# Cross-attention in eight chunks of keys a head: maxima in even steps, shifts computed on GpSimd, sums copied later

## The reference, cut to what matters

```python
q, k = _fq_sym(q, axis=-1), _fq_sym(k, axis=-1)      # 8-bit steps
v = _fq_sym(v, axis=2)
attn = softmax(einsum('bhqd,bhkd->bhqk', q, k))      # 16 heads, 896 queries, 24000 keys
attn = _fq_unsigned(attn, axis=-1)                   # round(255 * attn / max) * max / 255
out = einsum('bhqk,bhkd->bhqd', attn, v) @ Wp + bp
```

## Time and profile before

| | |
|---|---|
| median of 3 runs | 4739.06 us (4736.8 to 4739.14) |
| the profiled execution | 4743.85 us, its span 4740.7 us |
| TensorE clock granted | 0.986 of full over the span, 1.00 in the attention |
| busy over the span | PE 96%, VectorE 87%, ScalarE 76%, GpSimd 78% |
| one call of 192 steps | 221.2 to 223.4 us (14 calls from 966.5 to 4074.0 us) |

### The profile page before, as it was taken

How to read it: one execution, slowest core, us unless ns; L and a number is a source line. 1 busy time by engine, 2 the same in 40 slices (tenths; PEclk the granted TensorE clock), 3 DMA queues, 4 the chain that set the end, 5 groups by cost and what they waited for, 6 DMA issues and landing times. The chain is left out here.

```text
span 4740.7 us, 153131 instructions
## 1 busy us (share of the span) xinstructions
PE 4551.2 (96%) x55123; PEld 2083.6 (44%) x55123; DVE 4121.6 (87%) x7608; ACT 3614.3 (76%) x4027; POOL 3682.4 (78%) x3920
## 2 busy tenths in 40 slices
PE   7999998999999999999999999999999999888999
PEld 5666663333334443334343433333333434334655
DVE  6788888999999999999999999999999999874333
ACT  3555557888888898889888989888898988883121
POOL 5777777888889888888898989888898989872000
PEclk9999998999999999999999999999999999998999
DMA  3555541111111111111111111111111111342000
GB/s 99 150 160 166 172 148 52 31 32 35 32 34 31 35 34 33 32 34 33 33 35 35 31 32 35 35 31 34 33 34 32 34 33 32 128 164 92 1 37 8
DMA packets 222786, 268.95 MB, mean 57 GB/s; under 512 B 34367, under 2 KB 202810, under 8 KB 221290
## 3 DMA queue, kind: packets, MB, share of 16 engines
q1 hardware_dynamic: 167529, 203.57, 15.4%
q10 hardware_dynamic: 54528, 55.60, 3.8%
HBM read 174.57 MB, written 82.97 MB: 54 GB/s over the span
## 5 line engine op out<-in xcount | busy, mean ns | idle before, releaser
L1563 ACT ACTIVATE e_home<-ps_scores,sk 125x896 f32<-125x896 f32 x3072 | 3053.8, 1007 | 331.1 <-ACTq L1557 194.9
L1599 DVE TENSOR_REDUCE unit_max<-ps_maxima 128x1 f32<-128x428 f32 (+1 forms) x5880 | 3167.9, 599 | 86.7 <-DVEq L1596 64.7
L1771 POOL TENSOR_SCALAR r<-e_home 125x896 f32<-125x896 f32 x2976 | 2774.2, 949 | 418.9 <-ACT e_home L1563 221.3
L1354 PE MATMUL ps_maxima<-e_home,zt 126*17 126x224 f32 x24576 | 1708.9, 353 | 1.0 <-issue 1.0
L1332 PE MATMUL ps_maxima<-k_home,q 48*128 48x428 bf16 (+1 forms) x5880 | 1619.4, 345 | 41.0 <-PEq L1331 1.9
L1308 PE MATMUL ps_scores<-q,k_home 54*128 54x448 bf16 x5760 | 1591.5, 356 | 19.3 <-PEq L109 6.9
L1349 PE MATMUL ps_maxima<-r,vt 125*16 125x224 f16 x12288 | 853.4, 267 | 29.9 <-PEq L1342 25.3
L1308 PEld LDWEIGHTS ps_scores<-q,k_home 54*128 54x128 bf16 x5760 | 357.0, 94 | 980.4 <-issue 819.0
L1332 PEld LDWEIGHTS ps_maxima<-k_home,q 48*128 48x128 bf16 x5880 | 540.5, 93 | 282.9 <-issue 143.0
L1354 PEld LDWEIGHTS ps_maxima<-e_home,zt 126*17 126x17 f32 x24576 | 628.2, 96 | 3.7 <-issue 2.7
L1349 PEld LDWEIGHTS ps_maxima<-r,vt 125*16 125x16 f16 x12288 | 296.7, 85 | 742.6 <-issue 742.0
(11 more groups left out here) (269 smaller groups left out, 3009.5 us busy)
## 6 DMA issues: line engine op xcount, KB each, us to landing
k_rows<-krows ACTq DMA_DIRECT2D x48, 1000.0 KB, 7.2
k_home<-k_rows SPq DMA_DIRECT2D x408, 93.8 KB
k_home<-k_rows SPq DMA_DIRECT2D x120, 281.2 KB
e_home<-in_ctxT SPq DMA_DIRECT2D x48, 500.0 KB, 4.2
vr<-v_raw SPq DMA_DIRECT2D x128, 187.5 KB
cb<-in_ctxT SPq DMA_DIRECT2D x16, 1500.0 KB, 6.1
v_raw<-e_home SPq DMA_DIRECT2D x12, 1000.0 KB
v_raw<-vb SPq DMA_DIRECT2D x12, 1000.0 KB
```

Of the source, the lines that this page charges most:

```text
L1354: last = pe.matmul(psav[c:c + WIDE, lo:hi], zt[u][0:ONES_ROW + 1, i + s, :], e[(i + s) % SLOTS][0:ONES_ROW + 1, g, lo:hi], start=False, st ...
L1563: act.activation(e[i % SLOTS][0:KT, :, :], score_banks(i)[0:KT, :, :], ACT.Exp, scale=sk[u][:, i:i + 1]).then_inc(e_wrote[h % 2], 1)
L1599: top = dve.tensor_reduce(unit_max[:, b, j * NPIECE + at:j * NPIECE + at + 1], ps[:, 0:CUTS[at + 1] - CUTS[at]], axis=AX.X, op=ALU.max)
L1771: pool.tensor_scalar(r[i % SLOTS][:, :, :], e[i % SLOTS][0:KT, :, :], 1.0, HALFWORD, ALU.mult, ALU.add)\
```

## The change

- The seventh block of queries takes six pieces of 500 keys instead of seven of 428, so a chunk has 48 pieces and a head 384 (`place` gives each piece its block and cut, the 500-wide ones are every eighth). The 12 last steps hold 22 of the next head's pieces instead of 12. 362 remain for 180 steps: two steps have three pieces, the others two (24 in the first call with three).
- The maxima have two tiles, one for each parity of the head.
- The shift's arithmetic (eight operations) goes from VectorE to GpSimd, behind the rounding of i = 13 of chunk 7. VectorE keeps the reduction of the maxima. TensorE turns the rows in two parts at i = 20 and 22, ahead of the scores, and ScalarE copies them ahead of the exponentials of those steps. The banks that they use are freed by ScalarE's semaphores.
- The values are scaled at i = 1 and 4, rounded at i = 7 and 10, and added up at i = 14, 16 and 18.
- At the change of head TensorE no longer waits for the last sums. ScalarE copies the sums after the exponential of i = 4, and step 5 has no sums. At i = 6 TensorE waits for the copy and does both halves of the first pair, the f32 products first with `start` set, so that no clearing is needed. Semaphore `e_free` for the old head's last pair is given by the first score of i = 5.

```diff
-SB = 428
-NPIECE = CK // SB
-CUTS = [a * SB for a in range(NPIECE)] + [CK]
+NPIECE, NLAST = 7, 6
+CUTS = [a * 428 for a in range(NPIECE)] + [CK]
+CUTS_LAST = [a * 500 for a in range(NLAST + 1)]
...
-    UNITS = NQB * NPIECE
+    UNITS = (NQB - 1) * NPIECE + NLAST
-    EARLY = (1, 0, 1, 0, 1, 1, 1, 1, 1, 1, 2, 2)
+    EARLY = (1, 2, 2, 2, 2, 2, 2, 2, 1, 2, 2, 2)
+    SHIFTED = 8, 10
-    TURNED = len(EARLY) // 2
-    SCALED, WHOLE = (5, 8), (SLOTS + 2, SLOTS + 5)
+    SCALED, WHOLE, CHAINED = (1, 4), (SLOTS - 1, SLOTS + 2), 13
-    SUMMED, SUMMED_FIRST = (19, 20, 21), (1, 2, 3)
+    SUMMED, SUMMED_FIRST = (14, 16, 18), (1, 2, 3)
...
+        def place(n):
+            j, k = divmod(n, UNITS)
+            if k % 8 == 1:
+                return j, NQB - 1, j * NLAST + k // 8, CUTS_LAST[k // 8], CUTS_LAST[k // 8 + 1]
+            at, b = divmod(k - (k + 6) // 8, NQB - 1)
+            return j, b, j * NPIECE + at, CUTS[at], CUTS[at + 1]
...
+            def bank_free():
+                pe.wait_ge(shift_banks.get(turn.used - len(ps1), s1_free), 1)\
+                  .then_inc(shift_banks.get(turn.used - len(ps1), s1_free), -1)
...
-                if head_end:
+                if head_first:
+                    exact()
+                    last = products()
+                else:
+                    products()
+                    last = exact()
+                if final:
                     pe_done(last)
                     pe.sem_inc(e_free, 2)
                     pe.sem_inc(sums_done, 1)
+                elif head_end:
+                    last.then_inc(sums_done, 1)
...
-                    if head_start and i == LAG:
+                    if head_start and at == 0:
                         if finished is not None:
                             sums_read()
-                        clear_sums()
-                    if at >= 0:
+                        else:
+                            clear_sums()
+                        sums(0, u, 0, shared=not first, head_first=True)
+                        sums(0, u, 1, shared=not first, head_first=True)
+                    elif at >= 0:
...
+            def copy_shifts(half, ps, y, pair):          # ScalarE
+                lo, hi = ((0, BANK), (BANK, TOK))[half]
+                act.wait_ge(shift_turned, 1).then_inc(shift_turned, -1)
...
+                copied = act.activation(q2[y][0:SROWS, lo:hi], ps[0:SROWS, 0:hi - lo], ACT.Copy)
...
+            def turn_shift(h1):                          # GpSimd
+                pool.wait_ge(max_ready, 1).then_inc(max_ready, -1)
+                pool_done(pool.tensor_tensor(shift[:, :], run_max[:, :],
+                                             sq[:, :, bass.ds(h1, 1)].rearrange("p b o -> p (b o)"), ALU.mult))
+                pool_done(pool.tensor_scalar(shift[:, :], shift[:, :], -1.0, LOG255, ALU.mult, ALU.add))
+                for part in range(2):
+                    pool_done(pool.tensor_copy(shift_parts[:, :, part], shift[:, :]))
+                    rest = shift[:, :] if part == 0 else shift_parts[:, :, 2]
+                    pool_done(pool.tensor_tensor(rest, shift[:, :], shift_parts[:, :, part], ALU.subtract))
+                pool_done(pool.tensor_copy(shift_parts[:, :, 3:5], shift_parts[:, :, 0:2]))
+                pool.tensor_copy(shift_parts[:, :, 5], shift_parts[:, :, 0]).then_inc(shift_ready, 1)
...
+                    if n % NCH == NCH - 1 and i == CHAINED and n // NCH < HEADS - 1:
+                        turn_shift(n // NCH + 1)
```

More of the change, by code:

```diff
@@ L1321, in piece @@
             def piece(n, y):
-                j, at, b = n // UNITS, n % UNITS // NQB, n % NQB
+                j, b, _, lo, hi = place(n)
                 u = j % 2
@@ L1372, in clear_sums, with shift_rows @@
                               start=True, stop=True, tile_position=(0, g * QUAD))
[L1374 to L1384 removed]
+            def shift_rows(half, places):
+                if half == 0:
+                    pe.wait_ge(shift_ready, 1).then_inc(shift_ready, -1)
+                ps, lo = turn.next(), 4 * half
+                bank_free()
+                shift_banks[turn.used] = q2_ready if half else shift_copied
+                for at in places:
+                    for b in range(lo, min(lo + 4, NQB)):
+                        last = pe.matmul(ps[at:at + SROWS, (b - lo) * QB:(b - lo + 1) * QB], shift_parts[:, b, :],
+                                         ident_b[:, :], start=True, stop=True, tile_position=(0, at))
+                last.then_inc(shift_turned, 1)
             def sum_values(i, u, part):
@@ L1500, in chunk @@
                             sum_values(i, u if own else 1 - u, part)
+                        if j * CT + i - MAIN in SHIFTED:
+                            shift_rows(SHIFTED.index(j * CT + i - MAIN), (0,) if more else (0, ROWS1))
                         if second:
-                            score(i, 0, u, 1 - y)
+                            score(i, 0, u, 1 - y, head_ended=head_start and i == LAG and finished is not None)
                         for ahead, n in todo[:-1]:
@@ L1572, in chunk @@
                 def chunk(j, u, head_start, last):
-                    if h2 is None:
-                        return
                     for i in range(CT):
+                        if h1 is not None and j * CT + i - MAIN in SHIFTED:
+                            copy_shifts(SHIFTED.index(j * CT + i - MAIN), turn.next(), y, not more)
+                        for _ in pieces(j * CT + i, finished is not None, more) if h1 is not None else ():
+                            turn.next()
                         scores(h2, j, i, u, not head_start or finished is not None,
                                summed_at(j, i, h1 is not None, True, finished, last))
-                        if head_start and finished is not None and i == LAG - 2:
+                        if head_start and finished is not None and i == LAG - 1:
                             copy_sums()
@@ L1731, in chunk @@
                         if first and step == MAIN:
-                            head_max(h1)
-                        if first and step == MAIN + 1:
-                            high_part()
-                        if first and step == MAIN + 3:
-                            other_parts()
+                            dve.tensor_reduce(run_max[:, :], maxima[y][:, :, :], axis=AX.X, op=ALU.max).then_inc(max_ready, 1)
+                        if first and step - MAIN in SHIFTED:
+                            turn.next()
                         for ahead, n in todo:
                             piece(n, 1 - y if ahead else y)
-                        if first and step == MAIN + TURNED:
-                            shift_rows(y, not more)
                 over_chunks(chunk)
+            for u in range(2):
+                dve_done(dve.memset(maxima[u][:, NQB - 1, NCH * NLAST:], -3.0e38))
             for u in range(2):
```

95 lines of the change are left out of this document (45 added, 50 removed).

## The result

| | median, us | runs | over the kernel before |
|---|---|---|---|
| before, same chip | 4739.1 | 4 (4736.8 to 4741.16) | |
| after | 4700.73 | 4 (4698.44 to 4702.61) | 0.9919 (0.9902 to 0.9936) |

The change makes the kernel 38 us faster. The forecast was 102 us faster (4637) and its range ended at 4590 on one side and 4690 on the other, so the direction was right and the size far too large, by 64 us. The profiled execution has a span of 4696.0 us against 4740.7.

What follows compares the result with a forecast made beforehand. TensorE's own pace, 1.07 us a step, was taken as the bound. The terms summed to 7.1 us less a full call, 101.6 less than the profiled 4743.85, giving a median of 4637 us; range 4590 to 4690.

Steps and rivals of the forecast that it cites:

- the pieces: Steps with three pieces fall from 20 to two a full call, costing 1.0 us instead of 9.4: 8.4 less.
- Sums of values: Adding values up at i = 14, 16, 18 keeps ScalarE within its room: 2.5 us less a full call.
- Wide pieces: 500-column pieces outlast the score beside them on TensorE: 0.5 us more a full call, ends 0 and 1.4.
- The chain: GpSimd's eight shift operations take 3.9 us at i = 13 of chunk 7; TensorE waits 3.2 us a call.
- Change of head: Steps 4 to 6 of a call take 3.7 us together: 0.8 us less a call, ends 0 and 1.26.
- Shift copies: ScalarE copies the shift, 0.60 and 0.49 us: 0.5 us more a full call, ends 0 and 1.2.
- Values earlier: Value operations done by i = 10 make GpSimd late for i = 11: 0.4 us more a full call.
- The first call: Its steps with three pieces go from 32 to 24: 1.4 us less in all.
- B: Rival: the chain takes 2.6 us and side costs hide; 9.8 us less a full call, 4597 us, chance 0.22.
- C: Rival: VectorE's own pace of 0.534 us sets the step, four taking 4.34 us; 4681 us, chance 0.18.
- D: Rival: GpSimd's chain outweighs the gain, from a stop of 10.3 us; 4759 us at 1.5 a link, chance 0.05.

Runs made afterwards that it cites:

- e9: e5 with each 500-wide piece the first of its step instead of the second; 4658.26 us, 0.9825 of the kernel before.
- e6: Kernel after with the shift's eight operations back on VectorE at i = 12, 13 and 15, ScalarE still copying; 4740.56 us, 0.9998 of the kernel before.
- e8: Kernel after with the change of head as in the kernel before; 4714.54 us, 0.9944 of the kernel before.
- e10: e5 with sums of values at 16, 18, 20 and the shift turned at 21 and 23; 4647.28 us, 0.9803 of the kernel before.
- e7: Kernel after with the first six of GpSimd's eight shift operations done twice; 4761.01 us, 1.0039 of the kernel before.
- e5: Kernel after with the edits of e1 and e4 together; 4633.38 us, 0.9772 of the kernel before.
- e1: Kernel after with the values added up at i = 15, 17, 19 instead of 14, 16, 18; 4665.69 us, 0.9843 of the kernel before.
- e11: e10 with the second half of the values rounded at i = 11 instead of 10; 4632.79 us, 0.9775 of the kernel before.
- e4: Kernel after with 24 instead of 22 early pieces, so no step of a full call has three; 4683.87 us, 0.9876 of the kernel before.

## Why the prediction missed

- **What bounds the kernel, and the pieces: right.** TensorE's 1.07 us a step, three-piece steps at 1.57, eighteen of them gone.
- **Sums of values, "2.5 less": the step that failed**, in its sentence "The values are ready: GpSimd now rounds them at 7 and 10". The ScalarE half of the term held: steps 22 and 23 are plain. But the values are not ready, and TensorE stands 4.7 us a call for them. The prediction had nearly every number for it and applied them to the rounding of i = 11 and not to the values. By i = 10 GpSimd has done three value operations, 2 x 0.79 + 1.12 = 2.7 us, and regained 10 x 0.17: 1.0 late. From that step's start it takes 1.69 for the exponential, 0.08, 1.0, 0.90 for the rounding, and 0.85 and 0.28 for the values as measured above: ready at 4.8 (an estimate; 4.95 in the chunk shown). TensorE asks for them at the end of step 13, 3 x 1.07 + 0.97 = 4.2. So 0.6 us in each chunk, 0.74 in the one shown.
- **Wide pieces, "0.5 more": mis-sized, 2.3.** Its sentence "A wide piece that is the step's first has cover from what follows" had it the wrong way round (e9).
- **The chain, "3.2 more, the term that decides": mis-sized the other way, 1.7.** A link, from one start to the next, is 0.38 to 0.40 us, against 0.32 on VectorE: 0.21 for the operation and 0.17 to 0.20 for the wait, where 0.24 to 0.3 and 0.20 were taken. By these figures of its own (four products, four casts or copies, seven waits) the chain would have been 3.6 us; the 3.9 does not come out of them. The lower end, 2.6, was the nearer. The chain is 1.0 us shorter than forecast; the rest of the 1.5 is most likely the stop at step 13 itself, in which GpSimd catches up. The rule of the Trainium skill ("GPSIMD Engine Reference", section 4.1, Engine selection), about twice VectorE's time with two inputs, was applied to all eight operations, which gave the estimate of 5.2 us, though only three of them have two inputs. At seven columns the trace shows 1.2 times, with one input or two. And its advice, elementwise work to VectorE, costs 40 us here (e6): who waits behind an engine counted for more than the time of its operations.
- **Change of head, "0.8 less": right in the number, half by luck.** e8 gives 1.0, but steps 4 to 6 take 4.05 and not 3.7, which is 0.45 of the 0.8; the rest comes from a shorter wait at step 13, of which the term knew nothing. **Shift copies, "0.5 more": right**, steps 21 and 22 of chunk 7 at 1.33 and 1.44, 0.6 above plain, 0.3 of it TensorE's own. **Values earlier**: 0 in place of 0.4, see e10.
- **The first call** was to gain 1.4 and lost 1.6. Its step 13 takes 1.2 to 1.7 us in four of the eight chunks and 2.5 in one, and it had less to win. **The last full call** loses 8.5 us more than the others, and no term had that.
- **The rivals.** B had the chain and nothing else. C, VectorE's pace, is refuted where the wide piece is second: four steps take 4.30 there, and not 4.34. In chunks 0 to 3 they take 4.36, but e9 shows that it is the place of the wide piece that does this. D, GpSimd's chain outweighs the gain, was placed rightly and its threshold wrongly: e7 is slower than before at a stop of 4.4 us, not 10.3, since the rest of the gain was smaller by half and the clock adds to the stop; no rival had the clock.

Against the forecast for a full call: 4.7 for the values, 1.8 for wide pieces, less 1.5, 0.4 and 0.2, are 4.4 of the measured 3.7 (218.54 less 214.86). The 0.7 that is too much is within what so rough a sum can be off: the stop of the chain holds 0.3 of turning that is counted elsewhere too, and the change of head gave less where it was forecast. Of the 64 us by which the forecast was off, 57 show in the profiled executions (44.7 us faster instead of 101.6): 48 in the 13 full calls before the last, 12 in the last full call, 3 in the first, less 6 ahead of and behind these. That e5 runs in 4633, near 4637, doesn't make the forecast right: it is another kernel, and its terms are others.

**Left open.** Where e1's other 30 us went is seen by step: 1.6 us a call in steps 14 to 18 of chunks 0 to 6, and 1.2 in the rest of chunk 7, about a third of it the clock. Which wait takes the 1.6 was not looked at. The same holds for e10's and e11's chunk 7, whose steps 20 to 23 take 5.4 us, and for the slow roundings of the last full call. In e5, e10 and e11 step 13 of chunk 7 still takes 1.98 us: TensorE waits 0.57 for a bank while VectorE reduces the maxima (1.0 us with its wait) with two pieces in that step; with a single piece at i = 12 (e1) it takes 1.09, and step 14 takes 1.59 instead. An order that costs neither was not looked for.

## What to carry to other kernels

When a producer and its consumer move together on an engine that is nearly full, work out at the new place when the product is ready (how late the engine is there, plus all that stands before it) and when it is asked for; that it is issued some steps earlier says nothing. A gain ahead of such a wait is given back at it, so that two edits can be worth more together (e5, 67 us) than one by one (e1 and e4, 35 and 17). And a stop can cost more than its length: where TensorE's granted clock falls behind it, read the steps that follow by the clock before giving their length to a wait. And an order that alternates two sizes over a ring of buffers should be judged by who takes the buffer next, not by the longer operation.

## What the runs showed of the hardware

- TensorE's granted clock fell to 1.2 GHz behind single stops in a stream that was otherwise full. With 3.4 to 3.8 us idle (e7) it did so in each of the 13 full calls before the last, with 1.9 to 2.2 us (e6) in each of them too, with 1.64 to 1.70 us (e1) in 6 of 7, with 1.08 to 1.44 us (after) in one of 13, and not in e5, with at most 1.25 us. A fall cost 1.1 us in e1 and 1.4 us a call in e7, half as much again as the stop's growth.
- GpSimd's operations on 128 x 7 take 0.20 to 0.22 us each (product, cast, copy) outside the last full call; its casts of 64 columns took 494 ns in the trace before.
